# Closing the attention exponentials on GpSimd instead of VectorE, with sums and gates two blocks later

## The reference

```python
txt_proj = einsum('btd,de->bte', textual_features, Ws)
feat_proj = einsum('bfd,de->bfe', features, W)             # features = layernorm(x)
h = tanh(txt_proj[:, None] + feat_proj[:, :, None] + b)     # 4 x 1024 x 77 x 256 tanhs
rho = einsum('bftd,d->bft', h, w[:, 0]) + (1 - q_masks)[:, None] * NEG
att = softmax(rho, axis=-1)
txt_h = einsum('bft,btd->bfd', att, textual_features)
w_s = tanh(einsum('bfd,od->bfo', txt_h, Wcw) + bcw)
b_s = tanh(einsum('bfd,od->bfo', txt_h, Wcb) + bcb)
x = x + w_s * features + b_s
x = x + ffn(layernorm(x))    # a shared FFN, and 8 experts that take 512 tokens each by top-k
```

## Time and profile before

| what | us |
|---|---|
| median of three runs | 893.63 (891.44 to 894.2) |
| the profiled execution | 891.94 |
| its span, first to last instruction | 890.1 |
| PE busy | 799.7 (90%) |
| ACT busy | 759.5 (85%) |
| DVE busy | 714.6 (80%) |
| POOL busy | 308.1 (35%) |
| share of PE, ACT, DVE, POOL in the chain that ended last | 52%, 20%, 19%, 3% |

### The profile page before, as it was taken

How to read it: one execution, slowest core, us unless ns; L and a number is a source line. 1 busy time by engine, 2 the same in 40 slices (tenths; PEclk the granted TensorE clock), 3 DMA queues, 4 the chain that set the end, 5 groups by cost and what they waited for, 6 DMA issues and landing times.

```text
span 890.1 us, 14100 instructions
## 1 busy us (share of the span) xinstructions
PE 799.7 (90%) x5385; PEld 473.9 (53%) x5385; DVE 714.6 (80%) x1396; ACT 759.5 (85%) x589; POOL 308.1 (35%) x531
## 2 busy tenths in 40 slices
PE   6975679569998999989999999999988999999996
PEld 5321123124443444444444455555766999999986
DVE  5899888898889689997879996795887877676641
ACT  3989999999999999999998999997753677676672
POOL 3310540615543006775002650033403145555424
PEclk9899999999999999999999999999999999999999
DMA  8000000000001000200000010002202365544513
GB/s 261 25 1 0 1 1 1 1 24 1 25 1 48 1 1 25 71 1 2 24 1 1 24 49 1 24 1 97 71 24 78 105 174 142 143 106 126 138 19 41
DMA packets 32407, 41.82 MB, mean 47 GB/s; under 512 B 2366, under 2 KB 29012, under 8 KB 32340
## 3 DMA queue, kind: packets, MB, share of 16 engines
q1 hardware_dynamic: 26083, 32.49, 11.1%
q0 software_dynamic: 6144, 8.39, 5.8%
q10 hardware_dynamic: 112, 0.04, 0.0%
HBM read 28.33 MB, written 12.58 MB: 46 GB/s over the span
## 4 chain that ended last, share of the span: by engine, by line
PE 52%; ACT 20%; DVE 19%; issue 4%; POOL 3%; DMA 0%; POOLq 0%; DVEq 0%; ACTq 0%
ACT z L994 18%; PE bank L786 12%; DVE z L1375 11%; PE bank L913 10%; PE bank L936 9%; PE bank L843 7%; PE bank L828 6%; PE bank L762 2%; PE bank L714 1%; POOL xn L1139 1%; DVE att L1444 1%; PE bank L951 1%; ACT z L990 1%; PE bank L816 1%; PE bank L887 1%
## 5 line engine op out<-in xcount | busy, mean ns | idle before, releaser
L994 ACT ACTIVATE z<-z 128x4096 f32<-128x4096 f32 (+5 forms) x157 | 520.9, 3360 | 10.9 <-DVE z L1375 10.7
L1375 DVE TENSOR_SCALAR z<-feat,txt_bias 128x1024 f32<-128x1024 f32 (+1 forms) x722 | 417.9, 651 | 29.0 <-PE bank L786 28.1
L786 PE MATMUL bank<-z,window 128*32 128x512 f32 x2464 | 304.4, 604 | 63.0 <-ACT z L994 61.8
L786 PEld LDWEIGHTS bank<-z,window 128*32 128x32 f32 x2464 | 70.3, 110 | 247.8 <-issue 138.4
L843 PE MATMUL bank<-ws_sb,u 128*128 128x256 f32 x512 | 126.0, 387 | 1.5 <-ACT u L1043 1.5
L843 PEld LDWEIGHTS bank<-ws_sb,u 128*128 128x128 f32 x512 | 92.8, 190 | 35.5 <-issue 21.1
L828 PE MATMUL bank<-tr,ws_s 128*128 128x512 f32 x384 | 107.8, 417 | 2.8 <-issue 2.8
L1200 POOL TENSOR_TENSOR scale<-wb,x_ry 128x4 f32<-128x4 f32 x7 | 10.5, 1498 | 258.2 <-ACT wb L1005 258.2
L913 PE MATMUL bank<-xg_s,w_s 128*128 128x512 f32 x384 | 99.6, 397 | 0.2 <-DVE xg_s L1696 0.2
L936 PEld LDWEIGHTS bank<-w_s,hid_s 128*128 128x128 f32 x672 | 86.4, 188 | 4.0
L936 PE MATMUL bank<-w_s,hid_s 128*128 128x256 f32 x672 | 88.2, 280 | 0.0
(11 more groups left out here) (273 smaller groups left out, 780.1 us busy)
## 6 DMA issues: line engine op xcount, KB each, us to landing
w_raw<-in_L_ffn_W_dram SPq DMA_DIRECT2D x16, 1024.0 KB, 5.7
x_ring<-in_x_dram SPq DMA_DIRECT2D x8, 512.0 KB, 7.9
xn_dram<-xn SPq DMA_DIRECT2D x8, 512.0 KB, 2.9
out_dram<-x_ring SPq DMA_DIRECT2D x8, 512.0 KB, 3.0
u<-in_L_ffn_Ws_dram SPq DMA_DIRECT2D x1, 1024.0 KB, 11.5
ws_sb<-in_L_ffn_Ws_dram SPq DMA_DIRECT2D x1, 1024.0 KB, 14.2
xg<-xn_dram,idx POOLq DMA_INDIRECT x32, 4.4
out_dram<-y,idx POOLq DMA_INDIRECT x32, 3.9
```

Of the source, the lines that this page charges most:

```text
L786: ins = e.matmul(sums[v][32 * r:32 * r + 32, :], window[:, c, 31 - k:63 - k], z[:, n % ZB, at_piece:at_piece + TOK], start=(v, r) not in b ...
L994: e.activation(part, part, ACT.Tanh).then_inc(signal(*step), 1)
L1375: ins = e.tensor_scalar(z[:, n % ZB, i * width:(i + 1) * width], feat_of(units, c), bias_of(units, t, c), None, ALU.add)
```

## The change

`exp_close` of units 2 to 6 leaves VectorE's queue for GpSimd's. Its three operations become eleven, each waiting for the one before: 1 + t; a polynomial of second degree in it as a first guess of the reciprocal; two Newton steps of three operations; and the last scale. Six have one input tile (tensor_scalar), five have two (tensor_tensor). Its two scratch tiles are the halves of `att_tmp`, which `weigh` uses too, so it also waits for `weigh` of the unit before. The tables put `weigh`, `gate_in`, `y_scale` and `y_norm` of an early unit two slots later (`gates` two), `exp_close` of a late unit three slots earlier, and its `weigh` one later; for unit 6 `weigh` goes two slots later, `gate_in` and `gates` one. `y_turn` and everything that TensorE does keep their places.

```diff
-TAIL_EARLY = (0, 0, 1, 2, 3, 4, 4, 5, 4, 11, 6, 10, 12, 12, 14)
+TAIL_EARLY = (0, 0, 1, 2, 3, 6, 6, 7, 6, 11, 8, 10, 12, 12, 14)
...
-TAIL_LATE = (0, 1, 2, 3, 7, 8, 9, 10, 9, 13, 11, 15, 16, 16, 24)
+TAIL_LATE = (0, 1, 2, 3, 4, 9, 9, 10, 9, 13, 11, 15, 16, 16, 24)
-TAIL_SINGLE = (-1, 0, 1, 2, 3, 4, 5, 6, 9, 12, 10, 11, 10, 11, 13)
+TAIL_SINGLE = (-1, 0, 1, 2, 3, 6, 6, 7, 9, 12, 10, 11, 10, 11, 13)
...
+                elif kind == "exp_close":           # now in the queue of GpSimd
+                    v, = args
+                    a, near, rest_of = att[:, v % 2], att_tmp[:, 0], att_tmp[:, 1]
+                    e.wait_ge(*done("att_exp", v))
+                    e.wait_ge(*done("weigh", v - 1))
+                    link(e.tensor_scalar(a, a, 1.0, None, ALU.add))
+                    e.wait_ge(pool_link, linked)
+                    link(e.tensor_scalar(near, a, 32 / 99, -144 / 99, ALU.mult, ALU.add))
+                    e.wait_ge(pool_link, linked)
+                    link(e.tensor_tensor(near, near, a, ALU.mult))
+                    e.wait_ge(pool_link, linked)
+                    link(e.tensor_scalar(near, near, 210 / 99, None, ALU.add))
+                    for _ in range(2):
+                        e.wait_ge(pool_link, linked)
+                        link(e.tensor_tensor(rest_of, a, near, ALU.mult))
+                        e.wait_ge(pool_link, linked)
+                        link(e.tensor_scalar(rest_of, rest_of, -1.0, 2.0, ALU.mult, ALU.add))
+                        e.wait_ge(pool_link, linked)
+                        link(e.tensor_tensor(near, near, rest_of, ALU.mult))
+                    e.wait_ge(pool_link, linked)
+                    e.tensor_scalar(a, near, 2.0, -1.0, ALU.mult, ALU.add).then_inc(signal(*step), 1)
...
-                elif kind == "exp_close":           # was in the queue of VectorE
-                    v, = args
-                    a = att[:, v % 2]
-                    e.wait_ge(*done("att_exp", v))
-                    link(e.tensor_scalar(a, a, 1.0, None, ALU.add))
-                    e.wait_ge(vector_link, linked)
-                    link(e.reciprocal(a, a))
-                    e.wait_ge(vector_link, linked)
-                    e.tensor_scalar(a, a, 2.0, -1.0, ALU.mult, ALU.add).then_inc(signal(*step), 1)
```

## The result

The changed kernel takes 913.76 us (median of 4 runs, 913.04 to 915.49) against 892.58 us for the kernel before (891.44 to 894.2): a ratio of **1.0236, 95% interval 1.0214 to 1.0258**. That is 21.2 us more; the prediction said 15.9 us more, with a range of 896 to 919. The profiled execution has a span of 912.0 us against 890.1, so 21.9 us are to be found in the traces.

A forecast was written before the change was run, and what follows sets the result against it. TensorE was taken as full from unit 2's end to the last block. Losses of 6.6 us (first tail), 8.3 (second) and 1.0 (unit 6), together 15.9 on a median of 893.63, gave 909.5 us, range 896 to 919.

The forecast's parts named there:

- What bounds the kernel: From unit 2's end to the last block TensorE is full; relief of VectorE can give at most 7.5 us.
- The queue on GpSimd: Behind units 2 and 3, unit 3's exponential runs to 351 ahead of unit 2's scale; `y_turn` waits 9.7 us.
- The price of an operation for GpSimd: Exponential operations of 320 columns: 1.5 us each beside adds, 0.84 without; bounds 0.84 and 2.1.
- The loss of VectorE: VectorE's adds lose 0.15 us per GpSimd operation, 1.7 us per unit, against 2.88 saved.
- `y_norm` of unit 2: On GpSimd behind units 2 and 3, it ends at 363.6 us, after TensorE reaches `y_turn` at 353.87.
- What is given back behind the first tail: TensorE regains waits of 0.70, 1.59 and, at the next row's `x_turn`, part of 1.90; leaves +6.6 us at 400.
- The second tail: At `y_turn` of unit 4: 7.7 us late, less 1.91 of wait, plus 2.5 for the clock: +8.3 us.
- The clock: Behind each long TensorE wait at `y_turn`, the lower clock level costs 2.5 us.
- Unit 6: One exponential, gates one block later; nothing late, or 2.3 us if the first scale waits for a gap: +1 us.
- Rival 1: GpSimd's exponentials run at their free pace: 899 to 900 us; chance 0.14.
- Rival 2: VectorE's relief counts, with `y_norm` of unit 2 ending by some 356: faster, 889.5 us; chance 0.13.
- Rival 3: VectorE and GpSimd exclude each other for whole instructions: 920 us or more; chance 0.11, shared with a still slower GpSimd.

The follow-up runs named there:

- the ceiling test: Kernel before, places unchanged, with GpSimd closing each exponential by one operation in place of eleven, reciprocal left out: 891.73 us, ratio 0.9991.
- the kernel with the old places: Changed kernel with its exponentials on GpSimd, but all three place tables as in the kernel before: 926.57 us, ratio 1.0368.
- the one-input operations: Changed kernel with the five operations of two input tiles replaced by operations of one, reciprocal not computed: 908.23 us, ratio 1.0158.

## Why the prediction was right, and where it was off

It held: slower, by this mechanism, at these two places, within the range. It was 5.3 us short, and that it was not more is in part luck: two of its prices were wrong in opposite directions. By its own steps:

- **What bounds the kernel** was right, and more strictly than I dared say. The ceiling for a relief of VectorE was put at 7.5 us; the run with one operation in place of eleven shows some 2 at most, in the old order of the queues.
- **The queue on GpSimd** was right in kind and nearly in size. I had unit 2's exponential at 14.1 us of GpSimd's time; it took 12.3. Unit 3's was to run from 337.7 to 351 and ran from 340.20 to 353.17. The test with units 3 and 5 back on VectorE takes 10.3 us away.
- **The price of an operation for GpSimd** was taken at 1.5 us beside adds and is less: 1.13 to 1.14 us on average for the two-input ones, 0.68 to 0.73 for three of the five kinds of one-input ones. (The other two, L1219 and L1225, have one arithmetic step where the three have two, and L1219's mean holds a wait of 6.14 us.) All 55 took 61.3 us, and I had said 70 to 85. The five largest of the eight groups (count, busy us, mean ns, idle before):

```profile
L1228 POOL TENSOR_TENSOR att_tmp<-att,att_tmp 128x320 f32<-128x320 f32 x10 | 11.4, 1142 | 0.8
L1232 POOL TENSOR_TENSOR att_tmp<-att_tmp 128x320 f32<-128x320 f32 x10 | 11.3, 1133 | 0.8
L1219 POOL TENSOR_SCALAR att<-att 128x320 f32<-128x320 f32 x5 | 11.1, 2213 | 162.0 <-ACT att L1001 150.3 <-DVE wb L1471 11.7
L1225 POOL TENSOR_SCALAR att_tmp<-att_tmp 128x320 f32<-128x320 f32 x5 | 7.6, 1520 | 0.4
L1230 POOL TENSOR_SCALAR att_tmp<-att_tmp 128x320 f32<-128x320 f32 x10 | 7.3, 727 | 0.9
```

- **The loss of VectorE is the step that failed.** I took 0.15 us per operation, 1.7 us per unit, from adds beside one-input operations, and wrote that VectorE "has room in either case". One-input operations do cost about that (0.19), but five of the eleven have two inputs and cost 0.61 each. The loss is 4.2 to 4.3 us for each of units 2 and 3, more than the 2.88 us that VectorE is spared. I had "an operation lasts two adds"; here an operation and one add take turns (but for L1225, which lasts two). In the first tail it made the sums of unit 2 end at 340.1, not 337.7, and VectorE, which I had idle 4 us at unit 3's sums, waited 0.35. The errors in the two prices, GpSimd too slow and VectorE too fast, cancelled in part.
- **`y_norm` of unit 2** ended at 366.9 instead of 363.6: 2.4 us from the sums, 1.1 from the scale and the norm, which took 13.7 us and not 12.6, less 0.2 in unit 3's exponential and ahead of it. (The forecast's own terms for the scale, nine operations of 0.28 us and twelve of 0.55 from 351 on, end at 360.2 and not at its 359.7; 0.5 us of the 1.1 is that slip.) TensorE waited 12.57 us where I had 9.7.
- **What is given back behind the first tail**: 1.1 us less than I took. I let TensorE, 8.5 us late, run into an `x_turn` whose input was 4.7 us late. In the trace GpSimd's x_norm is late as well, and TensorE waited 1.12 of its former 1.90 us, so that it got back 0.8 us and not 1.9. So the first tail cost 10.9 us: 6.6, and 3.3 from `y_norm`, and 1.1 from here (0.1 is left over; the terms between were not measured one by one).
- **The second tail** cost 10.9 us instead of 8.3, with 10.76 us of wait instead of 7.7. I had taken 2 us off for adds of half the width, by analogy with the earlier trace rows, and they came: from the first scale to the end of xn it is 11.7 us here and was 13.7 in the first tail (GpSimd's timeline):

```profile
512.56 0.20 POOL L1200 TENSOR_TENSOR scale<-wb,x_ry 128x4 f32<-128x4 f32 x1
...
521.08 3.22 POOL L1139 TENSOR_SCALAR xn<-x_ring,y_ry,offset 128x256 f32<-128x256 f32 x4
```

  What was too small is what I carried over from the first tail. From the end of the unit's tanh (481.30) to the end of xn (524.30) it is 43.0 us, where I had 40.3.
- **The clock** was right: 2.5 us each in the sum, some 4 for both by experiment. The earlier trace rows were good rows for it.
- **Unit 6** cost nothing. The first operation did wait for a gap in the narrow adds, 6.14 us as in the earlier trace rows, but there was room.
- **Rival 1** (free pace) fell with the operations' 1.13 us. **Rival 2** (relief counts) fell with `y_norm` at 366.9, where it needed some 356, and with the ceiling test. **Rival 3** gave 920 or more by an exclusion for the whole instruction. The rows say that an add is lengthened by 0.19 or 0.61 us beside operations of 0.78 and 1.19 us; neither is the whole. The rule itself, from the Trainium skill (SBUF — State Buffer, Who interferes with whom), is that the losing side fully blocks for the whole of the other's instruction, and the trace does not agree with that for VectorE. The two losses are, though, each some 0.27 us less than what the operation takes where VectorE stands still (0.46 and 0.87 us), so, L1225 aside, an exclusion for all but a fixed part of an operation would give the same two prices. No run tells the two apart.

What the prediction did not do is price the change in two halves. It moved the gates two blocks later and counted that only inside GpSimd's queue. The experiment with the places alone shows that 10.2 of the 21.9 us come without any GpSimd exponential (with the one of unit 3 on VectorE ahead of unit 2's sums), and those of units 3 and 5 bring nearly all of the rest. The forecast's sum comes near because in the changed kernel both lie in one chain.

## What to carry to other kernels

Before moving work to an idle engine, ask what the work is worth where it stands (here some 2 us of 893 at most with the old order, as the kernel with one operation in its place showed) and what stands behind it in the other engine's queue: here a step on which the full engine waits. A step that is delayed to give the slow engine time has followers on three queues; here moving one of them moved the wait to the next, and moving all put them behind other waits. Price an elementwise operation on GpSimd beside VectorE's adds twice, once for each engine, and with its number of input tiles.

## What the runs showed of the hardware that was not expected

- VectorE's adds lose 0.19 us beside a one-input GpSimd operation of 320 columns and 0.61 beside a two-input one, and the two engines take turns, one add to one operation; L1225 lasts through two. The adds of half the width lose the same (0.48 us becomes 0.67 and 1.09 around 607 us). GpSimd's operation goes from 0.46 us (where VectorE stood still, in the kernel with the old places) to 0.78, and from 0.87 to 1.19.
- A tensor_scalar on GpSimd with one arithmetic step takes longer than one with two. L1219 and L1225, which only add a constant, take 1.03 and 1.02 us on 320 columns where VectorE stood still; L1221, L1230 and L1234, which multiply and add, take 0.46. Beside adds L1225 takes 1.62 and they take 0.78. On 4 columns beside adds it is 1.21 us (L1204 at 335.99 before) against 0.60 (L1113 at 339.94). Whether a second step that changes nothing would make the two of `exp_close` cheaper was not tried.
- Beside narrow adds (128x512) back to back, GpSimd's next operation can get no turn at all: 6.14 us for 320 columns in the changed kernel (the row below), and 8.54 us for 4 columns with the one-input operations. In the changed kernel the scale of unit 6 went through the same 28 adds in turns of 0.30 to 0.69 us and cost them nothing (11.17 against 11.18 us). What decides between the two is open.

```profile
596.60 6.14 POOL L1219 TENSOR_SCALAR att<-att 128x320 f32<-128x320 f32 x1 [56.82 <-ACT att L1001]
```

- Matmuls that compute nothing, put into a wait of 12 us, are worth 2 us per wait: the granted clock stayed at 1.00. If they are 5 us too long for each wait, they cost those 5 us each time: the span was 918.4 us with the long ones and 908.1 with the short.
